# Condition matrices loaded by pairs of rows, tokens split into even and odd channels

## The reference

```python
W = weights[condition]                         # (32, 64, 64), condition in 0..15
c = jnp.einsum('bct,bcd->bdt', x, W)           # (32, 64, 1024)
h = jax.nn.gelu(jnp.einsum('bsd,df->bsf', c, inter_w) + inter_b, approximate=True)   # 1024 -> 4096
out = x + jnp.einsum('bsf,fd->bsd', h, output_w) + output_b                          # 4096 -> 1024
```

## Time and profile before

| | us |
|---|---|
| median of 3 runs | 1261.15 (1261.07 to 1261.73) |
| the profiled execution, its own time | 1261.11 |
| its span in the trace | 1259.3 |
| TensorE busy | 1253.9 |
| VectorE, ScalarE, GpSimd busy | 830.7, 567.1, 186.2 |
| granted TensorE clock in the 40 slices of the page | 9 in each (90% of full speed or more) |
| DMA read and written | 162.28 MB and 85.98 MB, mean 197 GB/s |

### The profile page before, as it was taken

The page is one execution under the profiler, slowest core; times in us unless marked ns, Lnnn a source line. Parts: engine busy times, 40 slices in busy tenths (PEclk is TensorE's granted clock), DMA queues, the critical chain, the costliest instruction groups (busy, mean ns, idle before and its releaser), DMA issues.

```text
span 1259.3 us, 15367 instructions
## 1 busy us (share of the span) xinstructions
PE 1253.9 (100%) x5662; PEld 1043.5 (83%) x5662; DVE 830.7 (66%) x1090; ACT 567.1 (45%) x969; POOL 186.2 (15%) x93
## 2 busy tenths in 40 slices
PE   9999999999999999999999999999999999999998
PEld 9888888888888888888888888888888888888887
DVE  5977786776577777657656455554547767784764
ACT  4845454454544444444434434444444444444442
POOL 4262233321000000000034233322200000000000
PEclk9999999999999999999999999999999999999999
DMA  9486655864998223349835224554199932333431
GB/s 343 149 286 241 240 196 225 284 246 178 384 390 289 93 91 101 101 160 363 311 144 188 96 118 175 184 184 142 76 330 397 351 131 94 101 101 100 155 131 52
DMA packets 94090, 249.28 MB, mean 198 GB/s; under 512 B 7328, under 2 KB 15552, under 8 KB 92608
## 3 DMA queue, kind: packets, MB, share of 16 engines
q1 hardware_dynamic: 93408, 248.14, 54.6%
q10 hardware_dynamic: 576, 0.15, 0.1%
q0 software_dynamic: 32, 0.00, 0.0%
HBM read 162.28 MB, written 85.98 MB: 197 GB/s over the span
## 4 chain that ended last, share of the span: by engine, by line
PE 97%; DVE 1%; DMA 1%; SPq 0%; ACT 0%; issue 0%; ACTq 0%; DVEq 0%
PE ps L568 48%; PE ps L552 48%; DMA w_raw<-in_L_ffn_inter_w_dram 1%; PE ps L512 1%; DVE y_whole L783 1%; SPq L320 0%; DVE acc L866 0%; DVE lhs L788 0%; DVE y_whole L770 0%; DVE y L777 0%; ACT y_stage L609 0%; SPq L316 0%; ACT lhs L632 0%; SPq L317 0%; SPq L318 0%
## 5 line engine op out<-in xcount | busy, mean ns | idle before, releaser
L552 PE MATMUL ps<-y,lhs 128*128 128x512 f32 x2688 | 611.1, 389 | 0.0
L568 PE MATMUL ps<-rhs,lhs 128*128 128x512 f32 x2688 | 609.6, 389 | 0.0
L568 PEld LDWEIGHTS ps<-rhs,lhs 128*128 128x128 f32 x2688 | 504.5, 188 | 104.8
L552 PEld LDWEIGHTS ps<-y,lhs 128*128 128x128 f32 x2688 | 504.1, 188 | 104.5
L704 ACT ACTIVATE lhs<-h_raw 128x512 fp32r<-128x512 f32 x224 | 141.6, 632 | 345.9 <-PE ps L568 340.3
L847 DVE TENSOR_TENSOR lhs<-h_raw,lhs 128x512 fp32r<-128x512 f32 x224 | 155.2, 693 | 188.4 <-ACT lhs L704 188.4
L788 DVE TENSOR_TENSOR lhs<-w_raw,lhs 128x512 fp32r<-128x512 f32 x128 | 115.2, 902 | 127.2 <-ACT lhs L632 127.0
L632 ACT ACTIVATE lhs<-w_raw 128x512 fp32r<-128x512 f32 x128 | 80.9, 633 | 170.4 <-PE ps L552 164.4
L850 DVE TENSOR_TENSOR rhs<-W,rhs 128x512 fp32r<-128x512 f32 x224 | 153.4, 685 | 0.0
L788 DVE TENSOR_TENSOR lhs<-s_w,lhs 128x512 fp32r<-128x512 f32 x96 | 91.3, 953 | 89.6 <-ACT lhs L632 89.5
L465 POOL TENSOR_TENSOR s_w<-w_raw 128x1024 f32<-128x1024 f32 x16 | 48.5, 3030 | 620.6 <-PE ps L568 354.0
(11 more groups left out here) (34 smaller groups left out, 291.5 us busy)
## 6 DMA issues: line engine op xcount, KB each, us to landing
h_raw<-h_mem SPq DMA_DIRECT2D x112, 512.0 KB, 3.4
w_raw<-in_L_ffn_inter_w_dram SPq DMA_DIRECT2D x32, 1024.0 KB, 8.8
h_mem<-hs SPq DMA_DIRECT2D x64, 512.0 KB, 4.6
W<-in_L_ffn_output_w_dram SPq DMA_DIRECT2D x32, 1024.0 KB, 12.4
h_mem<-c SPq DMA_DIRECT2D x48, 512.0 KB, 5.5
y_mem<-y_out SPq DMA_DIRECT2D x28, 512.0 KB, 3.1
y<-y_mem SPq DMA_DIRECT2D x7, 2048.0 KB, 13.2
acc<-in_x_dram SPq DMA_DIRECT2D x16, 512.0 KB, 7.9
```

What stands on the lines that cost most here:

```text
L552: last = nc.tensor.matmul(ps[:, bank, :], w[:, k, :], y[i][:, part, k, :], start=(i in FRESH and k == 0 and u == 0), stop=(k == KH - 1 and ...
L568: last = nc.tensor.matmul(ps[:, bank2(h, j, tb), :], lhs[s % RING][:, a, blk(tb)], rhs[r][:, w, :], start=(j in FRESH and q == 0 and u == ...
```

## The change

- cond_all is loaded so that a partition holds two neighbouring rows of each condition matrix (512 bytes in a row); it takes 32 partitions and lies at another place.
- The partition order of x0 and x1 is now (channel parity, batch in the tile, channel pair): even channels in partitions 0 to 63, odd ones in 64 to 127. Each tile is loaded by two transfers of 64 partitions, and the upper half of the first half tile comes from ScalarE's queue. A block of wdiag is filled by two copies of 32 x 64. wdiag is zeroed whole, pass 0's half by VectorE and pass 1's by GpSimd.
- GpSimd fills tiles 0 to 4 of pass 1 ahead of its first sum of weights, and tiles 5 to 7 behind it. ScalarE waits for them in chunk 8, since cond_all lies where y5 goes.
- WARM is 10 instead of 15.
- y1_take(0) and y1_take(1) stand ahead of y_high(2).
- The last output tile is added and stored in two halves of 256 columns, the second by ScalarE's queue.

```diff
--- before.py
+++ after.py
...
     LAG = 5
-    WARM = 15
+    WARM = 10
     HRING = 4
...
+    x_con = x.rearrange("(h j s) (q r) t -> h j r (s q) t", h=PASSES, s=PER, r=2)
     out_tok = out.rearrange("(h j s) c t -> h (s c) j t", h=PASSES, s=PER)
-    cond_sets = cond_w.rearrange("s c d -> c s d")
+    cond_pairs = cond_w.rearrange("s (q r) d -> q s (r d)", r=2)
     w1_v = w1.rearrange("(k p) f -> p k f", p=P)
...
         y1_out = [at(f"y1_out{i}", 192 + 4 * i, [2, BANK], F32R) for i in range(2)]
-        cond_all = at("cond_all", 204, [SETS, C])[0:C]
+        cond_all = at("cond_all", 80, [SETS, 2 * C])[0:C // 2]
         wdiag = at("wdiag", 208, [PASSES * TILES, P])
...
         out_kept = [sem(f"out_kept{i}") for i in range(5)]
-        out_done = sem("out_done")
+        out_done, out_ended = sem("out_done"), sem("out_ended")
...
         ones_made = sem("ones_made")
-        wdiag_zero = sem("wdiag_zero")
+        wdiag_zero, wdiag1_zero = sem("wdiag_zero"), sem("wdiag1_zero")
         picked = [sem(f"picked_{e}") for e in ("pool", "act", "dve")]
...
-        TAKEN = (3, 3, 6, 6, 8, 8, 10, 12)
...
             which = engine.value_load(itok_sb[0:1, i:i + 1], min_val=0, max_val=SETS - 1)
-            rows = slice(s * C, (s + 1) * C)
-            return wdiag[rows, j:j + 1, rows], cond_all[:, bass.ds(which, 1), :]
+            cols = slice(s * C, (s + 1) * C)
+            return [(wdiag[(PER * r + s) * C // 2:(PER * r + s + 1) * C // 2, j:j + 1, cols],
+                     cond_all[:, bass.ds(which, 1), r * C:(r + 1) * C]) for r in range(2)]
...
+        ENDS = (slice(0, BANK // 2), slice(BANK // 2, BANK))
...
-            sp.dma_start(cond_all[:, 0:SETS // 2], cond_sets[:, 0:SETS // 2]).then_inc(cond_in, 16)
-            sp.dma_start(x0[:, 0, 0:BANK], x_tok[0, :, 0, 0:BANK]).then_inc(x0_half, 16)
-            sp.dma_start(x0[:, 0, BANK:D], x_tok[0, :, 0, BANK:D]).then_inc(x0_in[0], 16)
+            sp.dma_start(cond_all[:, 0:SETS // 2], cond_pairs[:, 0:SETS // 2]).then_inc(cond_in, 16)
+            sp.dma_start(x0[0:P // 2, 0, 0:BANK], x_con[0, 0, 0, :, 0:BANK]).then_inc(x0_half, 16)
+            for r in range(2):
+                sp.dma_start(x0[r * P // 2:(r + 1) * P // 2, 0, BANK:D], x_con[0, 0, r, :, BANK:D]).then_inc(x0_in[0], 16)
             for j in range(1, TILES):
-                sp.dma_start(x0[:, j, :], x_tok[0, :, j, :]).then_inc(x0_in[j], 16)
+                for r in range(2):
+                    sp.dma_start(x0[r * P // 2:(r + 1) * P // 2, j, :], x_con[0, j, r]).then_inc(x0_in[j], 16)
             load_w1(0, 0)
...
                     sp.wait_ge(cond_done, 2 * KB)
-                sp.dma_start(x1[j][:], x_tok[1, :, j, :]).then_inc(x1_in[j], 16)
+                for r in range(2):
+                    sp.dma_start(x1[j][r * P // 2:(r + 1) * P // 2], x_con[1, j, r]).then_inc(x1_in[j], 16)
             for j in range(TILES):
...
                 sp.wait_ge(acc_added, (2 * PRODUCTS - 1) * 2 + tb + 1)
-                cols = slice(n * BANK, (n + 1) * BANK)
+                cols = slice(n * BANK, (n + 1) * BANK) if tb < TB - 1 else ENDS[0]
                 sp.dma_start(out_tok[1, :, 4 * m + tb, cols], acc[:, 4 * m + tb, cols]).then_inc(out_done, 16)
...
             sp.wait_ge(out_done, 16 * (3 + TB))
+            sp.wait_ge(out_ended, 16)
...
             pool.dma_start(itok_sb[0:1], itok.rearrange("(o b) -> o b", o=1)).then_inc(itok_in, 16)
-            nc.gpsimd.memset(wdiag[0:C, :, C:P], 0.0).then_inc(wdiag_zero, 1)
-            nc.gpsimd.memset(wdiag[C:P, :, 0:C], 0.0).then_inc(wdiag_zero, 1)
+            nc.gpsimd.memset(wdiag[:, TILES:PASSES * TILES, :], 0.0).then_inc(wdiag1_zero, 1)
             pool.wait_ge(itok_in, 16)
             pool.wait_ge(cond_in, 32)
+            pool.wait_ge(wdiag_zero, 1)
+            pool.wait_ge(wdiag1_zero, 1)
             for i in range(0, TILES * PER, 3):
-                to, of = pick(pool, i)
-                nc.gpsimd.tensor_copy(to, of).then_inc(picked[0], 1)
-            pool.wait_ge(picked[0], 6)
+                for to, of in pick(pool, i):
+                    nc.gpsimd.tensor_copy(to, of).then_inc(picked[0], 1)
+            pool.wait_ge(picked[0], 12)
...
                 for i in range((TILES + first_j) * PER, (TILES + end_j) * PER):
-                    to, of = pick(pool, i)
-                    nc.gpsimd.tensor_copy(to, of).then_inc(picked1, 1)
-                pool.wait_ge(picked1, end_j * PER)
-            picks1(0, TILES)
+                    for to, of in pick(pool, i):
+                        nc.gpsimd.tensor_copy(to, of).then_inc(picked1, 1)
+                pool.wait_ge(picked1, 2 * end_j * PER)
+            picks1(0, TB + 1)
             for h in range(PASSES):
...
                     nc.gpsimd.tensor_tensor(s1_w[:], a21, a22, ALU.add).then_inc(s_made[0], 1)
+                    if n == 0:
+                        pool.wait_ge(s_made[0], 1)
+                        picks1(TB + 1, TILES)
                     if g > 0:
...
                 for j in range(n * TB, (n + 1) * TB):
-                    pe.wait_ge(x0_in[j] if j else x0_half, 16)
+                    pe.wait_ge(x0_in[j] if j else x0_half, 32)
                     for e in range(3):
-                        pe.wait_ge(picked[e], len(range(e, PER * (j + 1), 3)))
+                        pe.wait_ge(picked[e], 2 * len(range(e, PER * (j + 1), 3)))
                     for kb in range(KB):
                         if j == 0 and kb == KH:
-                            pe.wait_ge(x0_in[0], 16)
+                            pe.wait_ge(x0_in[0], 32)
                         if j == TB:
...
-                pe.wait_ge(x1_in[j], 16)
-                pe.wait_ge(picked1, PER * (j + 1))
+                pe.wait_ge(x1_in[j], 32)
+                pe.wait_ge(picked1, 2 * PER * (j + 1))
                 if j < 2:
...
                 nc.tensor.matmul(ps[:, i % 2, 0:P], ones[:, 0:P], ones[:, P:2 * P], start=True, stop=True)
-            pe.wait_ge(wdiag_zero, 2)
             for n in range(2):
...
-            act.dma_start(cond_all[:, SETS // 2:SETS], cond_sets[:, SETS // 2:SETS]).then_inc(cond_in, 16)
+            act.dma_start(cond_all[:, SETS // 2:SETS], cond_pairs[:, SETS // 2:SETS]).then_inc(cond_in, 16)
+            act.dma_start(x0[P // 2:P, 0, 0:BANK], x_con[0, 0, 1, :, 0:BANK]).then_inc(x0_half, 16)
             act.dma_start(b1_rows[0:F // P], b1.rearrange("(a p) -> a p", p=P)).then_inc(b1_in, 16)
...
             act.wait_ge(cond_in, 32)
+            act.wait_ge(wdiag_zero, 1)
             for i in range(1, TILES * PER, 3):
-                to, of = pick(act, i)
-                nc.scalar.activation(to, of, ACT.Copy).then_inc(picked[1], 1)
+                for to, of in pick(act, i):
+                    nc.scalar.activation(to, of, ACT.Copy).then_inc(picked[1], 1)
             y_keep(0)
...
                             high1(h, g, c)
+                        if (h, g, c) == (0, 0, 3):
+                            y1_take(0)
+                            y1_take(1)
                         if (h, g) == (0, 0) and c in (3, 5, 7, 8, 10):
+                            if c == 8:
+                                act.wait_ge(picked1, 2 * TILES * PER)
                             y_high({3: 2, 5: 3, 7: 4, 8: 5, 10: 6}[c])
                         if (h, g) == (0, 0):
-                            for j in range(TILES):
-                                if TAKEN[j] == c:
+                            for j in range(2, TILES):
+                                if BEHIND[j] + 3 == c:
                                     y1_take(j)
...
+            act.wait_ge(acc_added, 2 * PRODUCTS * 2 + TB - 1)
+            act.dma_start(out_tok[1, :, TILES - 1, ENDS[1]], acc[:, TILES - 1, ENDS[1]]).then_inc(out_ended, 16)
...
             nc.vector.memset(ones[:], 1.0).then_inc(ones_made, 1)
+            nc.vector.memset(wdiag[:, 0:TILES, :], 0.0).then_inc(wdiag_zero, 1)
             dve.wait_ge(itok_in, 16)
             dve.wait_ge(cond_in, 32)
+            dve.wait_ge(wdiag_zero, 1)
             for i in range(2, TILES * PER, 3):
-                to, of = pick(dve, i)
-                nc.vector.tensor_copy(to, of).then_inc(picked[2], 1)
+                for to, of in pick(dve, i):
+                    nc.vector.tensor_copy(to, of).then_inc(picked[2], 1)
             dve.wait_ge(b1_in, 16)
...
                             add_b2(h, q - 8)
-            for tb in range(TB):
+            for tb in range(TB - 1):
                 add2(1, 6, tb, 1)
+            dve.wait_ge(tile_done, TB)
+            for cols in ENDS:
+                tile = acc[:, TILES - 1, cols]
+                nc.vector.tensor_tensor(tile, ps[:, bank2(1, 6, TB - 1), cols], tile, ALU.add).then_inc(acc_added, 1)
...
```

## The result

| | before | after |
|---|---|---|
| median, us | 1261.11 (1260.91 to 1261.73, 6 runs) | 1269.30 (1267.45 to 1269.91, 6 runs) |
| profiled execution / its span | 1261.11 / 1259.3 | 1267.45 / 1265.6 |
| first product of TensorE starts | 21.57 | 25.63 |
| w1_raw0's first half lands | 19.36 | 23.92 |

The ratio is 1.0061, 95% interval 1.0051 to 1.0071: slower by 8.2 us, a small but clear difference. The forecast was 1259.7 in a range up to 1267.5, so both missed. Rival A's mechanism came true. First, three lines of the page of after: busy time, shares of the chain that ended last, and the first product's group with the idle time before it.

What follows compares the result with a forecast made beforehand. TensorE, busy 1253.9 of 1259.3 us, was taken as the bound, with w1_raw0's load and splits leading the first 37 us. Filler copies -1.17 and condition pairs -0.2, others 0, gave -1.4 on 1261.11: 1259.7 us, range 1258.9 to 1267.5.

Steps and rivals of the forecast that it cites:

- Rival A: x0's tiles ahead of w1_raw0: half loads run at 245 GB/s, w1_raw0 lands 7.0 later; +5.1, 1266.2 us; chance 0.32.
- Half loads: x0 and x1 in loads of 64 partitions: full rate of 414 GB/s, 1.27 us a tile, cost 0.
- The issues on SP: Sixteen more issues at 0.43 us, 0.95 per tile, under its 1.27; w1 load issued at about 9.5; cost 0.
- Fills in two copies: GpSimd's wdiag fills: second copy adds 0.23 us a block; last six blocks end at 30.2, before the second sum; cost 0.
- Rival C: GpSimd's fills at 1.4 us a block delay its sums and the product of chunks 4 and 5; 1263.9 us; chance 0.03.
- Filler copies sooner: Four copies moved into ScalarE's wait for VectorE remove TensorE's 0.97 us stall before cond1(2) and small later ones; -1.17 us.
- Ten ones: Condition product begins 0.9 us sooner, but waits for x0's tile 1 at 9.0 and ends at 21.5; gain 0.
- Rival B: TensorE idles from 5.6 to 6.3, its clock stays low, the condition product ends 0.7 later; 1260.4 us; chance 0.10.
- Condition pairs: Condition loads in 512 packets of 512 bytes: x0 and w1_raw0 behind them land 0.2 us sooner; -0.2 (0 to -0.44).
- Last tile split: Output's end: half an add sooner against one more add and 1 KB rows; 0, between -0.3 and +0.3 us.
- The range: Whole kernel: 1258.9 us (gains at their ends) to 1267.5 (most of Rival A); about 0.1 above, 0.05 below.
- list of signs: Expected in the trace: first product at 21.4, about 1.2 us less from there to 64.4, rows behind that unchanged.

Runs made afterwards that it cites:

- number 1: The kernel before, with each tile of x0 and x1 loaded by two transfers of 64 partitions: 1269.70 us, ratio 1.0068.
- number 2: The kernel before, with each tile of x0 and x1 loaded by two transfers of 128 partitions and half the columns: 1262.96 us, ratio 1.0014.
- number 3: The kernel after, with x0 and x1 loaded whole, 128 partitions a tile, in the old row order: 1262.83 us, ratio 1.0010.
- number 5: The kernel before, with only y1_take(0) and y1_take(1) moved ahead of y_high(2): 1259.64 us, ratio 0.9988.
- number 11: The kernel of number 5 with 10 ones matmuls instead of 15: 1259.89 us, ratio 0.9992.
- number 9: The kernel of number 3 with all 16 fills of pass 1 ahead of GpSimd's first sum of weights: 1261.45 us, ratio 1.0003.
- number 4: The kernel after, with 15 ones matmuls instead of 10: 1268.67 us, ratio 1.0061.
- number 7: The kernel before, with x0's tiles 1 to 7 loaded as all lower halves of the partitions, then all upper halves: 1270.61 us.
- number 8: The kernel before, with x0's lower halves loaded on SP's queue and its upper halves on ScalarE's: 1269.82 us.
- number 10: The kernel of number 3 with 15 ones matmuls: 1261.06 us, ratio 1.0000.
- number 6: The kernel before, with only the last output tile added and stored in two halves: 1261.35 us, ratio 0.9999.
- number 12: The kernel of number 5 with 5 ones matmuls instead of 15: 1263.43 us, ratio 1.0019.

## Why the prediction was wrong

- **Half loads, valued at 0:** this is the term that failed. It took 1.27 us a tile from the 414 GB/s of x0's packets, because the 245 GB/s of the condition loads could be explained by short packets. The runs gave 2.0 us a tile in after; numbers 1 and 2 put 6.7 to 8.6 us on the 64 partitions. Rival A had the place, the mechanism and the signs right. Its price of +5.1 is near the 6.3 between the profiled executions partly by luck: it put w1_raw0's landing at +7.0, and it was +4.56 (at 2.0 us a tile, not 2.14); it took 1.17 off for the fillers and nothing on behind the first product, where 3.16 were lost again to GpSimd's late sums. The other figure for rival A, 1268.3, lies near the median, but with 2.40 us a tile, which after didn't have. Only a chance of 0.10 had been given to a time over 1267.5.
- **The issues on SP, 0:** they took 0.60, not 0.43, and w1 was issued at 12.27, not 9.5. Still behind the queue in after, so 0 was right there. Number 2 has as many issues and lost 1.85, but whether by them or by its short rows isn't shown.
- **Fills in two copies, "hidden":** wrong in the pace at one of the two places. Ahead of the first sum a block takes 0.79 (five of them start at 5.01 to 8.19), less than the 0.93 assumed. Behind it the extra copy was taken as 0.23 again, and six blocks were to end at 30.2. The row of 0.23 was taken at 5.76, with VectorE nearly idle; behind the first sum VectorE is never idle. I had moved the fills without asking what runs beside them at the new place. Even with whole loads they end at 35.2 and hold the second sum to 35.29, which costs 1.63 (number 3). Rival C, at 0.03, had the second sum late, and 1.4 us a block against the measured 1.76, but for another reason (a second index load at every block) and with the first sum late as well, which it isn't in number 3 (21.54).
- **Filler copies sooner, -1.17:** right, with the reason given: -1.22 alone (number 5), -0.95 in after.
- **Ten ones, 0:** right in the total (number 11), wrong in the working. Tile 1 was put at 9.0 by the 6.3 from issue to landing in one execution; in number 11 it landed after 4.4, at 7.1, and the condition matmuls run from 5.94 to 20.5 without a wait. The product starts 0.91 earlier than before, but 0.59 of it number 5 has with 15 ones. Rival B's pause, behind the ones, did no harm with ten of them in the profiled executions of after and of numbers 3, 9 and 11, whose condition matmuls run at the full rate. With five the clock rises late, at a price of 1.4. The drops in numbers 4, 7 and 8 stand behind waits for data.
- **Condition pairs, -0.2:** not tried alone. In number 10, which has them, the first product starts at 21.16 against 21.57, but in number 5, which hasn't, at 20.98, so no gain of theirs can be read. No run shows the 0.2.
- **Last tile split, 0:** right (number 6).
- **The range:** the gains at their ends, 1.17, 0.44 and 0.3, give 1259.2, not the 1258.9 of its lower end; it changes nothing here.
- **The remainder:** the product at 64.36 moved by 6.27 and everything behind it kept its pace, as said in the list of signs.

**Open.** The profiled execution of after is 1.85 below its median, and its six runs stand in two groups, 1267.45 and 1267.72 against 1269.14 to 1269.91, so 1.85 of the 8.19 us are not explained. One candidate is the tail: the last loads of number 3 landed 1.9 us later than in before, and one of number 12 did. Number 12 has no split tail and number 6 has one without the delay; what makes it isn't known, and after's slower executions have no trace. The other candidate is a drop of the clock. The mean granted clock is 0.999, 0.998 and 0.999 in three of the four slower executions (1269.46, 1269.83, 1269.14) and 1.000 in the fourth and in the two faster ones. This doesn't decide: number 3's profiled execution has 0.999 by its low stretch behind the last matmul, number 4's by the stretch at 27 to 31 us, which cost nothing at the mark. Nor is it known why alternating halves ran at 264 in after, 234 in number 1 and 277 on two queues.

## What to carry to other kernels

Before splitting a load to suit a layout, look at its partition span as well as its packet length: here loads of half of the partitions ran at 0.51 to 0.67 of the full rate. Where a slow row in the trace has two possible explanations, don't forecast with the one that costs nothing; change one of the two and measure. A short instruction of GpSimd costs what stands beside it on VectorE, so read its duration at the place to which it moves. And where a change has many parts, the one with a named stall and a named cover (here a reordering of four copies) may be the only one worth keeping.

## What the runs showed of the hardware

- Loads of 4 KB rows: 414 GB/s to 128 partitions, 212 to 64 in one half, 234 to 277 with halves alternating or on two queues; the DMA engines are reported busy (1.00 to 1.04) in all of them. Loads of 2 KB rows to 128 partitions: 400, once under way (10 to 14 us of number 2).
- A 32 x 64 copy on GpSimd: 0.23 us, or 1.12 beside VectorE operations of two SBUF inputs.
- SP's issue of a load of 64 partitions took 0.60 us, of one of 128 partitions 0.43 to 0.73 in before (in the middle 0.56) and 0.43 to 0.71 in number 2 (0.45).
- One tile's load of 512 KB, issued at 2.7 us in both, landed after 6.3 us in before and after 4.4 in number 11.
- The granted clock fell to its lower level behind a pause of 2.55 us in number 4; after's profiled execution has a pause there too, of 2.40, and doesn't show it. In number 7 it was low from 12.5 to 22.7 us, while TensorE's wait of 8.31 us ended at 17.04.
- The last output loads landed after 2.1 us, in two profiled executions (numbers 3 and 12) after 4.0 or 4.1. In number 3 the mean granted clock of 0.999 comes from the time behind the last matmul.
- The granted clock is given as 1.00 while the first matmuls run at half pace (421 ns a record against 275 in number 12), so that stage has to be read from the pace.
